# Attention scores of a fused two-layer kernel: from six stacked bf16 piece products to three 32-bit ones, with two row groups of TensorE

## The reference, cut to what matters

```python
        k = (c_kv @ W_k_up).reshape(Bb, Tt, NH, HD)
        q = (x @ W_q).reshape(Bb, Tt, NH, HD)
        q_rope = _rotary_apply(x @ W_q_rope, cos, sin)
        scores = jnp.einsum('bqhd,bkhd->bhqk', q, k)
        scores = scores + jnp.einsum('bqr,bkr->bqk', q_rope, k_rope)[:, None]
        scores = scores / scale
        scores = jnp.where(causal[None, None], -jnp.inf, scores)
        w = jax.nn.softmax(scores, axis=-1)
        attn = jnp.einsum('bhqk,bkhd->bqhd', w, v).reshape(Bb, Tt, D_MODEL)
```

## Time and profile before

| | |
|---|---|
| median of 3 runs | 1405.07 us (1403.31 to 1408.92) |
| span of the profiled execution | 1405.9 us |
| PE busy | 1216.6 us, 87% |
| DVE busy | 1089.1 us, 77% |
| ACT busy | 1052.2 us, 75% |
| POOL busy | 333.9 us, 24% |
| mean granted TensorE clock | 0.936 of full speed |

### The profile page before, as it was taken

One profiled execution on the slowest core, in us unless ns is written; L12 is line 12 of the kernel. 1 busy time (PEld: TensorE's weight loads), 2 busy tenths in 40 slices (PEclk: granted clock), 3 DMA queues, 4 the chain that ended last, 5 costly groups with the idle time before them and its releaser, 6 DMA issues.

```text
span 1405.9 us, 23146 instructions
## 1 busy us (share of the span) xinstructions
PE 1216.6 (87%) x8060; PEld 778.2 (55%) x8060; DVE 1089.1 (77%) x2259; ACT 1052.2 (75%) x2103; POOL 333.9 (24%) x317
## 2 busy tenths in 40 slices
PE   5889885999899988998799989999899988977347
PEld 2575653465556754675556755666566655534224
DVE  3683388788788979889788989898688988887830
ACT  4675788797959878797859888788949887458522
POOL 3944110520133102320124112310133110510101
PEclk9799996999999999999999999999999999998669
DMA  8504141514142123521333041523151140031100
GB/s 254 113 9 102 27 130 42 115 31 116 46 102 72 23 75 88 126 46 41 98 91 82 24 128 28 132 44 103 38 120 38 26 131 28 23 96 50 37 0 15
DMA packets 72084, 101.65 MB, mean 72 GB/s; under 512 B 10640, under 2 KB 44064, under 8 KB 71968
## 3 DMA queue, kind: packets, MB, share of 16 engines
q1 hardware_dynamic: 71968, 100.16, 27.3%
HBM read 74.44 MB, written 25.69 MB: 71 GB/s over the span
## 4 chain that ended last, share of the span: by engine, by line
PE 54%; DVE 16%; ACT 16%; issue 6%; POOL 5%; SPq 1%; DMA 1%; POOLq 0%; DVEq 0%; ACTq 0%
PE ps L873 19%; PE ps L883 15%; PE ps L956 5%; DVE work L1516 4%; ACT work L1203 4%; PE ps L1042 4%; DVE work L1439 3%; PE ps L974 3%; PE ps L948 3%; ACT work L1210 3%; DVE work L1507 2%; ACT xnd L1146 2%; DVE work L1525 2%; PE ps L865 1%; DVE work L1394 1%
## 5 line engine op out<-in xcount | busy, mean ns | idle before, releaser
L1516 DVE TENSOR_TENSOR_SCAN work<-work 128x512 f32<-128x512 f32 x256 | 313.1, 1255 | 39.5 <-ACT work L1270 37.8
L1203 ACT ACTIVATE work<-work 128x384 f32<-128x384 f32 (+3 forms) x512 | 264.4, 559 | 54.6 <-DVE work L1439 52.7
L1439 DVE CUSTOM_DVE_ANT_0 work<-ps,work 128x384 f32<-128x384 f32 (+3 forms) x512 | 228.0, 486 | 90.8 <-PE ps L948 87.0
L752 POOL TENSOR_TENSOR later_norms<-later_norms,singles 128x2 f32<-128x2 f32 x112 | 97.0, 867 | 768.9 <-ACT xnd L1146 465.4
L956 PE MATMUL ps<-ident,work 128*128 128x128 f32 x1280 | 203.4, 285 | 21.4 <-DVE work L1439 10.2
L956 PEld LDWEIGHTS ps<-ident,work 128*128 128x128 f32 x1280 | 151.8, 145 | 84.5 <-issue 35.3
L1210 ACT COPY work<-ps 128x512 f32<-128x512 f32 x300 | 169.9, 573 | 7.8 <-PE ps L956 7.3
L1525 DVE TENSOR_TENSOR work<-work 128x1024 f32<-128x1024 f32 x128 | 160.0, 1250 | 4.3
L948 PE MATMUL ps<-work 96*128 96x384 bf16 (+3 forms) x512 | 124.1, 310 | 38.7 <-ACT work L1210 32.1
L873 PE MATMUL ps<-led_xTd,wf 128*128 128x512 f32 x256 | 120.3, 621 | 3.9 <-issue 3.9
L873 PE MATMUL ps<-led_xTd,wfc 128*128 128x512 f32 x256 | 118.0, 596 | 0.0
(11 more groups left out here) (176 smaller groups left out, 1950.7 us busy)
## 6 DMA issues: line engine op xcount, KB each, us to landing
work<-values SPq DMA_DIRECT2D x64, 256.0 KB, 3.1
work<-ratios SPq DMA_DIRECT2D x64, 256.0 KB, 3.2
scratch<-work SPq DMA_DIRECT2D x32, 384.0 KB, 4.7
work<-scratch SPq DMA_DIRECT2D x64, 192.0 KB, 3.9
work<-scratch SPq DMA_DIRECT2D x64, 128.0 KB, 4.2
x_in<-x SPq DMA_DIRECT2D x8, 512.0 KB, 6.7
work<-scratch SPq DMA_DIRECT2D x64, 64.0 KB, 4.3
values<-work SPq DMA_DIRECT2D x16, 256.0 KB, 3.2
```

Of the source, the lines that this page charges most:

```text
L1203: i = s_.activation(part_of, part_of, ACT.Exp, scale=-1.0, bias=nmax[:, row:row + 1])
L1439: i = v_.tensor_tensor_reduce(sc[:, n % 4, at:at + nk], out_of(b, name)[:, at:at + nk], base_of(qt), -SCORE_SCALE, BIG, ALU.add, ALU.min, ...
L1516: v_.tensor_tensor_scan(ring[:, at, m, :], pwr[:, slot, :], ring[:, at, m, :], 0.0, ALU.mult, ALU.add).then_inc(*scanned.one)
```

## The change

The split of q and k is now in two 32-bit pieces (`float32r`), the leading one written by ACT and the remainder by DVE straight from PSUM; POOL has no part in it. A score is the sum of three piece products over 48 rows. Of the four heads of a group two lie on partitions 0 to 47 and two on 64 to 111, so that the matmuls of two consecutive units go to different halves of the rows of the array. `attention_items` now emits `T` n-3 ahead of a pair `S` n, `S` n+1 (n even). The units of 256 columns now pair heads j and j+2. The pieces of q lie in `xna` and in the space of `base`, so the first `base` of a batch on DVE waits for the DMAs that send them. The `MERGE` tables of all five engines are new. Number, width and order within their chains of all other items are the same.

```diff
-RUNS = (((0, 3), (0, 3)), ((0, 2), (1, 2)), ((0, 1), (2, 1)))
-SROWS = 6 * HD
+SROWS = 3 * HD
+SGROUP = P // 2
 
 TILES = ([((3, j, 0),) for j in range(4)] + [((2, j, 0), (0, j, 3 * P)) for j in range(4)] +
-         [((1, j, 0), (1, j + 1, 2 * P)) for j in (0, 2)])
+         [((1, j, 0), (1, j + 2, 2 * P)) for j in (0, 1)])
...
-        if n < ALL:
-            items.append(("S", n))
+        if LAG_T <= n < ALL + LAG_T:
+            items.append(("T", n - LAG_T))
+        if n < ALL and n % 2 == 0:
+            items += [("S", n), ("S", n + 1)]
         if n in (UNITS + 1, 2 * UNITS + 1):
             items.append(("group", n // UNITS + 1))
-        if LAG_T <= n < ALL + LAG_T:
-            items.append(("T", n - LAG_T))
...
 MERGE = {
     "pe":
-        "a5 p a3 p a6 p4 a34 p a24 p a31 p3 a6 p a p a p a p a p a5 d a2 d a2 d a4 d6 a3 d a6 d a3 d a6 d a12 "
...
+        "a8 p a2 p a4 p4 a29 p a6 p a21 p a3 p2 a10 p2 a11 p a3 p a7 p a14 d a3 d a d2 a3 d a d2 a3 d a3 d a3 d "
...
     "pool":
-        "a p a4 p8 a3 d2 a4 d15 a3 d2 a4 d16 a7 d18 a3 d4 a2 d a2 d17 a d4 a2 d2 a4 d16 a d4 a2 d2 a4 d20 a7 "
-        "d22 a2 d34",
+        "a p9 a3 d17 a3 d14 a d4 a2 d18 a3 d22 a d3 a2 d19 a d3 a2 d19 a d4 a2 d22 a2 d34",
...
-        k_pieces = part(3 * DC * T // 2).bitcast(BF16).rearrange("p (c s t) -> p c s t", s=3, c=DC)
+        k_pieces = part(2 * DC * T).bitcast(F32R).rearrange("p (c s t) -> p c s t", s=2, c=DC)
...
-        rest = xna[:].rearrange("p t d -> p (t d)").rearrange("p (c t) -> p c t", c=DC)
+        q_pieces = [a.bitcast(F32R).rearrange("p (s t) -> p s t", s=2)
+                    for a in (xna[:].rearrange("p t d -> p (t d)"), base[:, 0:2 * T])]
...
-                i, at = hg % 2, 0
-                for run in RUNS:
-                    for kind in range(2):
-                        s0, k = run[kind]
-                        sp.dma_start(stack[at:at + k * HD, i, kind].rearrange("p j t -> p (j t)"),
-                                     scratch[b, kind, hg % 2, hg // 2, s0:s0 + k]
-                                     .rearrange("s (d j) t -> (s d) (j t)", j=4)).then_inc(*stacked[i].one)
-                    at += k * HD
+                i = hg % 2
+                for kind in range(2):
+                    for h in range(2):
+                        sp.dma_start(stack[h * SGROUP:h * SGROUP + SROWS, i, kind].bitcast(F32).rearrange("p j t -> p (j t)"),
+                                     scratch[b, kind, hg, h, 0:SROWS].rearrange("r j t -> r (j t)")
+                                     ).then_inc(*stacked[i].one)
...
-                    need(sp, third_piece, b, (n + 1) * DC)
-                    pieces = (q_pieces, k_pieces)[n]
-                    for half in range(2):
-                        r = half * 64
-                        sp.dma_start(scratch[b, n, half].rearrange("c s r t -> r (c s) t"),
-                                     pieces[r:r + 64].rearrange("p c s t -> p (c s) t")).then_inc(*pieces_sent.one)
+                    for c in range(DC):
+                        is_drained(sp, b, f"{'qk'[n]}{c}")
+                        pieces = k_pieces[:, c] if n else q_pieces[c]
+                        for to, of, k in [(0, 0, 1), (1, 0, 2)] if n == 0 else [(0, 0, 2), (2, 0, 1)]:
+                            rows = scratch[b, n, 2 * c:2 * c + 2, :, to * HD:(to + k) * HD].rearrange(
+                                "g h (s d) j t -> (g h) (d j) s t", s=k)
+                            for s0 in range(k):
+                                sp.dma_start(rows[:, :, s0], pieces[:, of + s0].bitcast(F32)).then_inc(*pieces_sent[n].one)
...
-                if item in ("q", "k"):
-                    pieces, pick = (q_pieces, (1, 2)) if item == "q" else (k_pieces, (1, 0))
-                    is_drained(pool, b, f"{item}{n}")
-                    pool.sem_inc(waits_taken, 1)
-                    g_.tensor_copy(pieces[:, n, pick[0], :], rest[:, n, :]).then_inc(*second_piece.one)
-                    need_given(pool, second_piece)
-                    g_.tensor_tensor(pieces[:, n, pick[1], :], rest[:, n, :], pieces[:, n, pick[0], :],
-                                     ALU.subtract).then_inc(*third_piece.one)
...
                     for qt, j, at in TILES[n % UNITS]:
                         nk = (qt + 1) * P
-                        i = mm(out_of(b, name)[:, at:at + nk], stack[0:SROWS, hg % 2, 0, j, qt * P:(qt + 1) * P],
-                               stack[0:SROWS, hg % 2, 1, j, 0:nk], start=True, stop=True)
+                        of = stack[j % 2 * SGROUP:j % 2 * SGROUP + SROWS, hg % 2, :, j // 2]
+                        i = mm(out_of(b, name)[:, at:at + nk], of[:, 0, qt * P:(qt + 1) * P], of[:, 1, 0:nk], start=True, stop=True)
...
                     name, at = f"base{n}", n * P
+                    if n == 0:
+                        need(dve, pieces_sent[0], b, 3 * DC)
                     is_filled(dve, b, name)
```

More of the change, by code:

```diff
@@ L10 @@
 I32 = mybir.dt.int32
-BF16 = mybir.dt.bfloat16
+F32R = mybir.dt.float32r
 P = 128
@@ L161 @@
            "osum gystats ternary prep tables means late",
-    "pool": "stats q k ystats fstats fc fystats zstats oystats gstats gystats gsum ternary tables late",
+    "pool": "stats ystats fstats fc fystats zstats oystats gstats gystats gsum ternary tables late",
     "sp": "fetch pieces group z kv ratio rates pw inv gsum",
@@ L168 @@
     "pe":
[11 rows of a table removed]
-    "act":
[16 rows of a table removed]
-    "dve":
[13 rows of a table removed]
[11 rows of a table added]
+    "act":
[16 rows of a table added]
+    "dve":
[15 rows of a table added]
     "pool":
[2 rows of a table removed]
+        "a p9 a3 d17 a3 d14 a d4 a2 d18 a3 d22 a d3 a2 d19 a d3 a2 d19 a d4 a2 d22 a2 d34",
     "sp":
[3 rows of a table removed]
+        "a3 d a11 d3 m6 d2 m7 a3 m a2 m3 a2 d2 m d m3 d m9 a5 m2 a m2 d3 a d3 m4 d m7 a m2 a4 m a m3 d3 a d3 m4 "
+        "d m9 a5 m a m3 d3 a d3 m4 d m9 a5 m a m3 d3 a d2 m d m4 d m8 a5 m a m3 d3 a d2 m2 d m5 d m10 d6 m4 d "
+        "m13 d4",
 }
@@ L383, in sandwich_kernel @@
         means = sb("means", [P, 4, TT])
-        words = 28864
+        stack = ctx.enter_context(nc.sbuf_tensor("stack", [P, 2, 2, 2, T], F32R))
+        words = 24768
         work = sb("work", [P, words])
@@ L400, in part @@
             return ap.rearrange(f"p ({' '.join(names)}) -> p {' '.join(names)}", **dict(zip(names, shape)))
-        stack_at = cut[0]
-        stack = part(2 * 2 * 4 * T // 2).bitcast(BF16).rearrange("p (i k j t) -> p i k j t", i=2, k=2, j=4)
-        cut[0] = stack_at + 2 * 4 * T // 2
-        q_pieces = part(3 * DC * T // 2).bitcast(BF16).rearrange("p (c s t) -> p c s t", s=3, c=DC)
-        cut[0] = stack_at + 2 * 2 * 4 * T // 2
         base = part(TT * (TT + 1) // 2 * P)
@@ L457, in sandwich_kernel @@
         first_piece = signal("first_piece", 2 * DC)
-        second_piece = signal("second_piece", 2 * DC)
-        third_piece = signal("third_piece", 2 * DC)
-        pieces_sent = signal("pieces_sent", 4, 16)
-        stacked = [signal(f"stack{i}_loaded", 2 * 2 * len(RUNS), 16) for i in range(2)]
+        pieces_sent = [signal(f"{kind}_pieces_sent", 3 * DC, 16) for kind in "qk"]
+        stacked = [signal(f"stack{i}_loaded", 2 * 2 * 2, 16) for i in range(2)]
         exped = signal("exped", ALL)
@@ L686, in do @@
                 if item == "pieces":
-                    need(sp, third_piece, b, (n + 1) * DC)
-                    pieces = (q_pieces, k_pieces)[n]
-                    for half in range(2):
-                        r = half * 64
-                        sp.dma_start(scratch[b, n, half].rearrange("c s r t -> r (c s) t"),
-                                     pieces[r:r + 64].rearrange("p c s t -> p (c s) t")).then_inc(*pieces_sent.one)
+                    for c in range(DC):
[6 more added lines that the diff above has]
+                                sp.dma_start(rows[:, :, s0], pieces[:, of + s0].bitcast(F32)).then_inc(*pieces_sent[n].one)
                 if item == "group":
                     if n < 2:
-                        need(sp, pieces_sent, b, 4)
+                        need(sp, pieces_sent[0], b, 3 * DC)
+                        need(sp, pieces_sent[1], b, 3 * DC)
                     else:
@@ L943, in do @@
                     if n % UNITS == 0:
-                        need(pe, stacked[hg % 2], b, (hg // 2 + 1) * 2 * len(RUNS))
+                        need(pe, stacked[hg % 2], b, (hg // 2 + 1) * 4)
                     may_fill(pe, b, name)
@@ L1188, in do @@
                     is_filled(act, b, f"q{n}")
-                    s_.copy(q_pieces[:, n, 0, :], out_of(b, f"q{n}")).then_inc(*first_piece.one)
+                    s_.copy(q_pieces[n][:, 0, :], out_of(b, f"q{n}")).then_inc(*first_piece.one)
                 if item == "k":
                     is_filled(act, b, f"k{n}")
-                    s_.copy(k_pieces[:, n, 2, :], out_of(b, f"k{n}")).then_inc(*first_piece.one)
```

(15 more changed lines are left out.)

## The result

| | median | lowest to highest |
|---|---|---|
| before, beside it | 1405.51 us (4 runs) | 1403.31 to 1408.92 |
| after | 1673.34 us (4 runs) | 1672.19 to 1678.77 |

A forecast was written before the change was run, and what follows sets the result against it. TensorE was taken to bound the attention stretch: +45 for shape changes less 9 for overlap is +36 us, 70% showing as +25, less 5 at the start, +20 on the span: median 1425 us, range 1383 to 1475.

The forecast's parts named there:

- Part 5: Piece DMAs and DVE's first `base` waiting for q's pieces: nothing, hidden; 7 us over the batches if 1 us showed.
- Part 1: Score columns on TensorE: a 32-bit product of 512 columns streams in 0.22 us, as bf16; 0.43 kept for the range.
- rival 1: Score products on TensorE: the 32-bit record streams at 0.43 us, giving 1460 us, up to 1492; chance 0.17.
- Part 2: Paired score units on different array rows overlap, limited by matmuls starting in order: gain 8.6 us, 14 without that limit.
- Part 3: Array shape changes around 48-row scores: 350 more in batches 1 to 7 at 0.13 us, 45 us; bounds 0 and 70.
- the share of 70%: How much of TensorE's added 36 us in the middle shows in the time: 70%, from 54% to 83%, so +25 us.
- Rival 2: Between T and S: half the rows is no shape of its own, or its switch is hidden; 1385 us, chance 0.27.
- Rival 3: The cost is real but falls into PE's 82 us of idle in the middle: 1405 to 1412 us, chance 0.14.
- Part 4: POOL's casts and subtractions go, so the start, before the first S, is 5 us shorter; bounds 0 and 7.6.
- Part 6: Waits for banks, T behind a pair, in the new order: nothing, left to the range at some 10 us either way.
- Rival 4: Waits for banks or q's pieces make T or `base` late by 1 us per batch and group: 35 us, 1460; chance 0.05.

The follow-up runs named there:

- experiment 1: The changed kernel with a head's rows ordered channel first, piece second, so each piece DMA writes 64 outer rows instead of 4: 1478.9 us, ratio 1.053.
- experiments 1 and 3: The third adds to experiment 1 before's item order and tables (1468.28 us), S on 96 rows summing two heads (1441.61 us), or both (1416.74 us).
- Experiment 6: 96-row kernels with the mixer's Sin replaced by Exp: new order 1432.76 us, old order 1408.93; separately, with Sin, before's item list under the new tables: 1525.66 us.

## Why the prediction was wrong

**Part 5 is the step that failed.** It put q's and k's pieces at nothing, "a landing took 4.7 us: hidden", under 8.0 us of cover. The landing was read from DMAs of 384 KB over 64 outer rows and carried to DMAs of 256 KB over 4. Bytes and count were compared, the shape was not, though the changed code has `(g h)`, which is 4, outermost. In place of a hidden landing the runs show a phase of 34.6 us a batch, with 82 us of DVE's waits for q's pieces and 166 us of TensorE's idle time behind it. The place was right (q's pieces before `base`, then the group), and the Part even names it as the cover that could be gone, at 1 us a batch. Over the 8 batches the true price is 194 us, 24 a batch. With 64 outer rows "hidden" comes true: in experiment 1 DVE waits for q's pieces in batch 0 only. The sum of the step had a smaller gap too: it named the six issues and gave them no time. In before's trace one takes about 0.6 us, so six of them, the subtraction of 0.69 and a landing of 4.7 are 9 us against 8.0 of cover; that experiment 1 hides them rests on its shorter landing, 2.6.

**Part 1 holds.** The 32-bit product streams at 0.22 us for 512 columns, and rival 1 is out. The test I set for it was bad: "a lone S of 512 takes 0.43" is just what after shows (at 932.87 below), but as 0.22 of columns and 0.21 of entry. Only the run on 96 rows, 0.24, tells the two apart. What Part 1 missed is the weight load, 0.19 against 0.10 us, worth some 10 us.

**Part 2 has the overlap right, but not its rule and not how often it comes.** Chain of after. At 379.60 stand two units of 256 and 256 columns, at 610.11 two of 384 and 128, at 932.87 one matmul of 512, and at 949.15 two of 512, on different rows:

```profile
379.60 0.44 PE ps L937 x4
...
610.11 0.43 PE ps L937 x4
...
932.87 0.43 PE ps L937
933.29 0.59 PE ps L853 x4
...
949.15 0.43 PE ps L937 x2
```

Two units take no longer than one, in all three forms. The prediction gave the last two forms only 0.05 and 0.11 us, since "matmuls start in order". The records say otherwise for different halves of the rows: the 384 columns of the second unit start 7 ns after those of the first, ahead of the first unit's 128, which stand before them in the program and start 0.28 us after them. But of the 65 pairs counted in batches 1 to 7 only 26 ran side by side in after. In the other 39 the second unit started 0.3 to 5.6 us late, and in 28 of these PE idled in between, 29 us in all. The two errors partly cancel: 26 x 0.21 is some 5 us of gain in place of 8.6.

**Part 3 had the mechanism right and its term too small.** It took 0.13 us a change, the low middle of 0.12 to 0.20; entry is 0.19 to 0.21 and return 0.14 to 0.19 (T 0.59, dense 1.91). TensorE's busy time differs by 43 us between 48 and 96 rows in the new order (1284.3 and 1241.6, the gain of Part 2 in it), where Parts 2 and 3 had 36. Of the 43, 37 show in the medians and 34 in the spans of the profiled executions: 80% to 87%. In the old order it is 61 (1299.7 and 1238.5), and 52 and 44 show, 71% to 84%. So the cost was low and the share of 70% at the low end, and the product was +37 instead of +25. Rival 2 is refuted: T behind S takes 0.59. Rival 3 too: the cost does not fall into the idle time.

**Part 4's 5 us at the start did not come.** In the run on 96 rows in the old order, whose DMAs spread over the engines, the first S stands at 46.1 us, as in the earlier trace rows at 45.16, and in the other runs of experiments 1 and 3 at 42.8 to 46.8, not near 41; in after at 68.4. POOL is indeed 63 us less busy. What took the gain at the start was not tried.

**Part 6 was no zero.** The new order costs some 11 us with half rows and 25 without; "some 10 us either way" was half wide enough. Experiment 6 shows it as waits and a lower granted clock; which waits make it stays open.

The loss of 268 us, taken down in steps: 194 for the DMAs on four engines (1673 to 1479), 37 for the shape (1479 to 1442), 25 for the order (1442 to 1417), and 14 for the rest of the pieces (1417 to 1403), 10 of them with the 32-bit weight loads. The split between shape and order depends on which goes first: the other way round it is 11 for the order and 52 for the shape. The prediction's +36 on PE at 70% was an account of the second alone. Rival 4 had this wait, `base` late, at under a fifth of its size (35 us).

## What to carry to other kernels

A DMA whose layout changes is a new DMA: before its landing time is taken over from a row, compare the outermost dimension of its view with the row's, and look at the share of the DMA engines, not only at bytes and count. A matmul on 48 or 64 rows between neighbours on the whole array pays at both sides, some 0.35 us a visit here with 32-bit pieces and 0.25 with bf16, while one on 96 rows paid nothing. One visit costs more than the 0.21 us that a pair saves side by side. Standing together in the order is not enough for a pair either: the bank of the second has to be free. A criterion for a rival has to be a number that the forecast excludes.

## What the runs showed of the hardware

- A DMA with an outermost dimension of 4 ran at a share of 0.26 of the 16 engines, 102 GB/s, with many queued behind it; with 64 rows the same bytes ran at 0.79 to 1.02, 298 to 352 GB/s. With many DMAs queued, SP's own issue stretched from 0.58 to 2.44 us, and all that was behind it on SP waited.
- The one-pass 32-bit product streams 512 columns in 0.22 to 0.24 us, as bf16; its weight load takes 0.190 us where bf16 takes 0.098.
- A change from the whole array to 48 rows costs 0.19 to 0.21 us, and back 0.14 to 0.15 before a transpose; for a bf16 product of 64 rows 0.10 and 0.15. Going to 96 rows costs nothing (0.22 us for 512 columns of bf16 in before).
- Matmuls on different halves of the rows run fully side by side: two of 512 columns take 0.43 us, as one does (0.21 of it entry), and so do two units of 384 and 128 or of 256 and 256 (0.43 and 0.44). There a later matmul of the program starts before an earlier one of the other half.
- When TensorE had stood still (882 to 887 us), its granted clock fell from 1.0 (2.4 GHz) towards its lower level of 1.2 GHz (mean 0.57 from 887 to 910 us), which made its busy time 47 us longer over the program (1331.7 and 1284.3 us, or 1205 and 1209 when multiplied by the granted clock).
